# Turning the normalised rows of the second half on VectorE and through DRAM instead of on TensorE

## The reference

```python
h = _layernorm(x) * (1 + ca) + sa
x = x + ga * attention(h)          # q, k, v, rope, causal softmax, output projection
h = _layernorm(x) * (1 + cb) + sb
# ffn, for flat = h.reshape(2048, 512):
logits = flat @ router_weight.T + router_bias
scores = softmax(logits)
topk_w, topk_idx = top_k(scores, 8)
w_sum = topk_w.sum(-1, keepdims=True)
out = flat * w_sum + w_dense @ expert_bias
x = x + gb * out
```

## Time and profile before

| | |
|---|---|
| median of 3 runs | 1455.2 us (1454.89 to 1455.63) |
| profiled execution | 1455.76 us, span 1454.5 us |
| granted TensorE clock | 0.999 of full speed |
| busy, share of the span | PE 1432.3 us (98%), PEld 1210.8 (83%), DVE 1150.7 (79%), ACT 1008.6 (69%), POOL 1024.5 (70%) |
| DMA | 322.05 MB, mean 221 GB/s |

### The profile page before, as it was taken

The page is one execution under the profiler, slowest core; times in us unless marked ns, Lnnn a source line. Parts: engine busy times, 40 slices in busy tenths (PEclk is TensorE's granted clock), DMA queues, the critical chain, the costliest instruction groups (busy, mean ns, idle before and its releaser), DMA issues.

```text
span 1454.5 us, 24712 instructions
## 1 busy us (share of the span) xinstructions
PE 1432.3 (98%) x7150; PEld 1210.8 (83%) x7150; DVE 1150.7 (79%) x3541; ACT 1008.6 (69%) x2391; POOL 1024.5 (70%) x806
## 2 busy tenths in 40 slices
PE   7999999999999999999999999999999999999998
PEld 7887888888888888888888888888888888888886
DVE  5697777777877777777777787777779988898876
ACT  5686767667676666677676677677667676776674
POOL 3776866677676667677676677676588888887662
PEclk9999999999999999999999999999999999999999
DMA  9487667776666766676587668659878899888972
GB/s 307 164 238 236 223 185 201 240 219 187 185 219 199 214 211 217 195 219 195 179 234 218 213 182 219 191 174 267 229 231 261 270 293 262 284 248 277 269 233 68
DMA packets 215158, 322.05 MB, mean 221 GB/s; under 512 B 42512, under 2 KB 132464, under 8 KB 215024
## 3 DMA queue, kind: packets, MB, share of 16 engines
q1 hardware_dynamic: 214736, 320.39, 73.5%
q10 hardware_dynamic: 288, 0.07, 0.0%
HBM read 179.43 MB, written 140.95 MB: 220 GB/s over the span
## 4 chain that ended last, share of the span: by engine, by line
PE 87%; DVE 5%; POOL 3%; ACT 2%; issue 2%; DMA 1%; SPq 0%; DVEq 0%; ACTq 0%
PE bank_s L642 22%; PE bank_o L804 21%; PE bank_pv L766 14%; PE bank_s L708 13%; PE bank_s L674 5%; PE bank_s L659 5%; POOL PT_lo L1890 1%; PE bank_s L704 1%; PE bank_s L613 1%; PE bank_s L868 1%; DVE y L1581 1%; DVE blocks L1529 1%; PE bank_s L705 0%; POOL rot_c L1878 0%; DMA wc_scratch<-wc_out 0%
## 5 line engine op out<-in xcount | busy, mean ns | idle before, releaser
L1890 POOL TENSOR_TENSOR PT_lo<-PT_raw,PT_hi 128x640 fp32r<-128x640 f32 x247 | 384.2, 1577 | 29.1 <-ACT PT_hi L1152 29.1
L1138 ACT ACTIVATE probs<-probs,row_inv 128x512 f32<-128x512 f32 (+3 forms) x512 | 257.6, 553 | 195.0 <-DVE row_inv L1512 194.9
L1878 POOL TENSOR_TENSOR rot_c<-rot_c,rot_s 128x512 f32<-128x512 f32 x128 | 167.3, 1307 | 256.5 <-DVE rot_s L1469 256.5
L1131 ACT ACTIVATE probs<-probs,row_min 128x384 f32<-128x384 f32 (+3 forms) x512 | 281.6, 552 | 50.6 <-DVE row_min L1505 50.5
L1529 DVE STREAM_TRANSPOSE blocks<-probs 128x384 f32<-128x384 f32 x508 | 213.9, 447 | 22.4 <-ACT probs L1138 13.1
L708 PE MATMUL bank_s<-kT_both,qT_hi 128*128 128x512 f32 (+2 forms) x768 | 215.2, 341 | 1.7 <-issue 1.1
L1505 DVE CUSTOM_DVE_ANT_0 probs<-bank_s,mask 128x512 f32<-128x512 f32 (+2 forms) x384 | 205.3, 552 | 0.3
L1883 POOL TENSOR_TENSOR qT_lo<-rot_c,qT_hi 128x512 fp32r<-128x512 f32 x128 | 166.3, 1299 | 51.4 <-ACT qT_hi L1113 50.6
L804 PE MATMUL bank_o<-wo_lo,OT_hi 128*128 128x512 f32 x496 | 195.0, 393 | 0.0
L642 PE MATMUL bank_s<-hT_lo,wq_hi 128*128 128x512 f32 x480 | 193.5, 403 | 0.5
L804 PE MATMUL bank_o<-wo_hi,OT_hi 128*128 128x512 f32 x496 | 193.4, 390 | 0.0
(11 more groups left out here) (311 smaller groups left out, 3198.3 us busy)
## 6 DMA issues: line engine op xcount, KB each, us to landing
blocks<-blocks SPq DMA_DIRECT2D x127, 640.0 KB, 3.7
PT_raw<-blocks SPq DMA_DIRECT2D x500, 160.0 KB, 3.9
stage<-in_wq SPq DMA_DIRECT2D x32, 256.0 KB, 5.1
vblocks<-kv_raw SPq DMA_DIRECT2D x32, 256.0 KB, 5.4
kv_raw<-vblocks SPq DMA_DIRECT2D x128, 64.0 KB, 2.2
stage<-in_wo SPq DMA_DIRECT2D x32, 256.0 KB, 5.1
split_wq<-wq_hi SPq DMA_DIRECT2D x32, 256.0 KB, 5.4
split_wq<-wq_lo SPq DMA_DIRECT2D x32, 256.0 KB, 5.7
```

The lines of the kernel that those rows point to most:

```text
L1131: ins = act.activation(row(t, qt), row(t, qt), ACT.Exp, bias=row_min[m][:, qt:qt + 1], scale=-1.0, accum_out=row_sum[m][:, qt:qt + 1])
L1138: ins = act.activation(row(t, qt), row(t, qt), ACT.Copy, scale=row_inv[t % 2][:, qt:qt + 1])
L1878: pool.tensor_tensor(rot_c[:], rot_c[:], rot_s[:], ALU.add).then_inc(pool_a, 1)
L1890: pool.tensor_tensor(lo[:, at], raw_of(t)[:, at], hi[:, at].bitcast(F32), ALU.subtract).then_inc(pool_t, 1)
```

## The change

The four transposes of each of the 12 tiles leave TensorE. VectorE turns the normalised rows in 32x32 blocks (`turn_rows`) in the odd step after, SyncE stores them to a DRAM buffer (`store_turned`) and reads them back with the blocks in their places by four loads (`load_turned`). ScalarE modulates out of SBUF (`modulate_turned(n-2)`), a tile one even step later than before, at the same place. TensorE's logits move to the end of the even step, behind the values products, always into bank s1; the bias moves to the start of the next odd step on VectorE.

```diff
@@ tensor_program: scores, step
-                    if before is not None and logits_bank(t - 2) == f"s{qt}":
-                        tile_waits((bias, before - 2), last=EARLY_TILES - 1)
                     if qt == 1 and t - 2 in MOD_STEPS:
                         pe.wait_ge(dve_mod, MOD_READ[MOD_STEPS[t - 2]])
                     if qt == 1 and before is not None:
-                        tile_waits((h2T_copy, before - 1), last=EARLY_TILES - 1)
+                        tile_waits((mixed, before - 4), (bias, before - 2), last=EARLY_TILES - 1)
...
                 if n is not None:
                     pe.wait_ge(dve_s, score_read(t + 1, 0))
                     ffn_mix(early(n - 4), "s1")
-                    ffn_logits(early(n - 2), logits_bank(t))
                 if h % 2 == 0 and t > 2:
                     out_pair(t // 2 - 2, LOWER)
-                if n is not None:
-                    tile_waits((mixed, n - 4), last=EARLY_TILES - 1)
-                    ffn_transpose(early(n - 1), "s1")
                 if h % 2 == 0 and t > 0:
                     if t < ALL - 2:
                         values_pair(t // 2 - 1, UPPER)
                     else:
                         values_last_pair()
+                if n is not None:
+                    tile_waits((mixed, n - 4), last=EARLY_TILES - 1)
+                    ffn_logits(early(n - 2), "s1")
@@ scalar_program
+            def modulate_turned(i):
+
+                if 0 <= i < TILES:
+                    b = i // QT
+                    act.wait_ge(d_turned, TURNED * (i + 1))
+                    act.wait_ge(d_modT, COLUMNS)
+                    if i > 0:
+                        act.wait_ge(logits_done, i)
+                    hidden = turned[:].rearrange("p (i c a) -> p c i a", i=SUBS, a=SUB)
+                    for c in range(CH):
+                        ins = act.activation(h2T(i)[:, c * P:(c + 1) * P].rearrange("p (i a) -> p i a", a=SUB),
+                                             hidden[:, c], ACT.Identity,
                                              bias=modT_rows[:, 0, b, c:c + 1], scale=modT_rows[:, 1, b, c:c + 1])
                     ins.then_inc(h2T_copy, 1)
...
                 if n is not None:
-                    ffn_modulate(early(n - 1), "s1")
+                    modulate_turned(early(n - 2))
@@ vector_program
+            def turn_rows(i):
+                if 0 <= i < TILES:
+                    dve.wait_ge(normed, i + 1)
+                    if i > 0:
+                        dve.wait_ge(h2T_copy, i)
+                    dve.transpose(turned[:].rearrange("p (j c a) -> p c j a", j=SUBS, a=SUB),
+                                  normal[:].rearrange("p (c j b) -> p c j b", j=SUBS, b=SUB)).then_inc(transposed, 1)
...
+                if before is not None:
+                    ffn_bias(early(before - 2), "s1")
                 mask_and_max(t + 1, 0)
...
                 if before is not None:
+                    turn_rows(early(before - 1))
                     ffn_x1(early(before))
                     ffn_stats(early(before))
...
                     ffn_top(early(n - 3))
-                    ffn_bias(early(n - 2), logits_bank(t))
                     keep(early(n - 3))
@@ sync_program
+            def store_turned(i):
+                if 0 <= i < TILES:
+                    sp.wait_ge(transposed, i + 1)
+                    sp.dma_start(turned_d, turned[:]).then_inc(d_turned, 16)
+
+            def load_turned(i):
+                if 0 <= i < TILES:
+                    sp.wait_ge(d_turned, TURNED * i + 16)
+                    rows = turned_d.rearrange("(i b) (j x) -> j b i x", b=SUB, j=SUBS)
+                    for j in range(SUBS):
+                        to = turned[j * SUB:(j + 1) * SUB, :].rearrange("p (i x) -> p i x", i=SUBS)
+                        sp.dma_start(to, rows[j]).then_inc(d_turned, 16)
...
                     if 1 < t < ALL - 3:
                         load_transposed(t - 1)
+                    if ffn_tile(t - 1) is not None:
+                        store_turned(early(ffn_tile(t - 1) - 1))
                     load_transposed(t)
...
                 if moved(t + 1):
                     store_blocks(t + 1)
+                if ffn_tile(t - 1) is not None:
+                    load_turned(early(ffn_tile(t - 1) - 1))
```

More of the change, by code:

```diff
@@ L274, in build @@
         x_end = [gate1[1], shift2[1], scale2[1], Region(fourth[0]).take("x_end3", [P, HID])]
+        turned = Region(fourth[0]).take("turned", [P, HID])
         x_in = stage[0]
@@ L343, in build @@
         vblocks_d = [nc.dram_tensor(f"vblocks{i}", [P, SEQ], F32).ap() for i in range(2)]
+        turned_d = nc.dram_tensor("turned_scratch", [P, HID], F32).ap()
         v_raw = kv_raw[:].rearrange("p (i k a) -> p k i a", i=SUBS, a=SUB)
@@ L359, in q_bank @@
             return bank["pv" if t < 5 else {5: "o3", 6: "o3", 7: "pv"}.get(t, "s2" if third_first(t - 2) else "s3")]
-        def logits_bank(t):
-            return "s3" if third_first(t + 1) else "s2"
         def k_bank(u):
@@ L477, in build @@
         act_pro, act_comb, act_h = sem("act_pro"), sem("act_comb"), sem("act_h")
-        dve_pro, dve_mod, dve_ln, dve_xn, dve_h = (sem("dve_pro"), sem("dve_mod"), sem("dve_ln"), sem("dve_xn"),
-                                                   sem("dve_h"))
+        dve_pro, dve_mod, dve_ln, dve_h = sem("dve_pro"), sem("dve_mod"), sem("dve_ln"), sem("dve_h")
+        d_turned = sem("d_turned")
+        TURNED = 16 + 16 * SUBS
         act_xn = sem("act_xn")
@@ L1190, in ffn_modulate @@
                     act.wait_ge(d_modT, COLUMNS)
-                    if 0 < i < EARLY_TILES:
-                        act.wait_ge(logits_done, i)
                     if i == EARLY_TILES + 2:
@@ L1197, in ffn_modulate @@
                         ins = act.activation(h2T(i)[:, at], bank[ps][:, at], ACT.Identity,
+                                             bias=modT_rows[:, 0, b, c:c + 1], scale=modT_rows[:, 1, b, c:c + 1])
+                    ins.then_inc(h2T_copy, 1)
+            def modulate_turned(i):
[9 more added lines that the diff above has]
+                                             hidden[:, c], ACT.Identity,
                                              bias=modT_rows[:, 0, b, c:c + 1], scale=modT_rows[:, 1, b, c:c + 1])
@@ L2235, in load_column @@
                 sp.dma_start(to, src.rearrange("(c p) -> p c", p=P), allow_slow_non_contiguous=True).then_inc(d_modT, 16)
+            def store_turned(i):
[9 more added lines that the diff above has]
+                        sp.dma_start(to, rows[j]).then_inc(d_turned, 16)
             def load_end(j):
                 sp.wait_ge(shifted, 2 * QT)
+                if j == QT - 1:
+                    sp.wait_ge(h2T_copy, EARLY_TILES)
                 sp.dma_start(x_end[j][:], x_rows[EARLY_TILES + j]).then_inc(d_xend, 16)
```

## The result

| | before | changed |
|---|---|---|
| median of 6 runs each | 1455.81 us (1454.89 to 1457.78) | 1463.33 us (1460.08 to 1465.6) |
| ratio, with 95% interval | | 1.005 (1.0039 to 1.006) |
| span of the profiled execution | 1454.5 us | 1462.1 us |

The change makes the kernel 7.5 us slower. Forecast were 1461.2 us and slower by 0.4%; it is 0.5%, inside the range and inside rival A's own range.

What follows compares the result with a forecast made beforehand. The prediction took a dense TensorE stream as the bound, other engines finishing just in time. Its terms -5.0 + 8.3 + 2.7 = +6.0 gave 1461.8 us profiled, 1461.2 us as median, range 1454.5 to 1467.

Steps and rivals of the forecast that it cites:

- rival A: Logits on TensorE wait for ScalarE at t mod 4 = 2; 1458.5 to 1464.5 us; chance 0.56, the forecast itself.
- The transposes, -5.0: On TensorE, removing the four transposes of each of 12 tiles saves 0.42 us a tile, 5.0 us.
- rival E: Each transpose costs TensorE its whole 272 ns, so 13.1 us come back; with waits 1453.1 us; chance 0.03.
- The logits' wait, 8.3: TensorE waits before the logits for ScalarE's modulation in five steps of t mod 4 = 2, adding 8.3 us.
- The wait for GpSimd, 2.7: Values products, coming 1.30 us earlier, wait for GpSimd's low parts near t = 96, 112, 116, adding 2.7 us.
- VectorE's odd step, +0.22: Block transpose adds 0.67 us, an earlier start gives back 0.45: VectorE's odd step moves 0.22 us against TensorE.
- The DMAs, nothing: The store and loads of turned rows lie hidden beside other work: no cost, upper bound 6 us.
- Rival B: The transfer becomes a bound: half a microsecond more for each of 12 tiles, 1467 us; chance 0.19.
- Rival C: Late TensorE gives GpSimd and VectorE time: GpSimd wait vanishes, logits' wait halves, about 1455.5 us; chance 0.15.
- Rival D: Faster: transposes go and ScalarE reaches the modulation early enough everywhere, 1450.2 us; chance 0.07.

Runs made afterwards that it cites:

- Experiment 8: Kernel before without the 12 tiles' transposes, ScalarE modulating straight from untransposed normalised rows, logits at their old place: 1451.11 us, ratio 0.9965.
- experiment 1: Changed kernel with ScalarE's modulation moved ahead of the key split in steps t mod 4 = 2: 1454.49 us, ratio 0.999 to the kernel before.
- experiment 6: Changed kernel with one 512-column activation for the modulation instead of four of 128: 1458.35 us, ratio 1.0012 to the kernel before.
- experiment 11: Changed kernel with VectorE's small two-source subtraction replaced by a one-source instruction with accumulator: 1461.07 us, ratio 1.0042 to the kernel before.
- experiment 2: Changed kernel with VectorE adding the logits' bias ahead of the output's low part: 1463.96 us, ratio 1.0056 to the kernel before.
- experiment 7: Changed kernel with VectorE turning only 32 of 512 columns in tiles 1 to 11: 1461.32 us, ratio 1.0038 to the kernel before.
- experiment 5: Changed kernel without the DRAM store and four loads of the turned rows: 1461.66 us, ratio 1.0037 to the kernel before.
- experiment 10: Changed kernel with the modulation ahead of the key split and no DRAM store or loads of turned rows: 1454.24 us, ratio 0.9992 to the kernel before.
- experiment 9: Changed kernel with the modulation ahead of the key split and VectorE turning only 32 columns in tiles 1 to 11: 1452.33 us, ratio 0.9982.

## Why the prediction was right, and where it was not

The steps of the profiled executions by kind, t = 94 to 119, changed minus before:

| steps | forecast | measured |
|---|---|---|
| t mod 4 = 2 (94 to 118) | 8.3 - 6 x 0.42 = +5.8 | +5.5 |
| t mod 4 = 0 (96 to 116) | 2.7 - 6 x 0.42 = +0.2 | -0.5 |
| odd (95 to 119) | 0 | +4.4 |
| sum | +6.0 | +9.4 |

(With t = 119 the sum is 9.4; up to its start, the stretch, it is 8.6. The rest of the execution was 1.8 us shorter than in the profile of before: the part ahead of t = 94, whose code did not change, by 2.0, of which 1.6 are the fall of the clock at t = 5 that the profile of before holds. The profiles of the experiments have the start of t = 94 between 1048.98 and 1051.91 us. Without the two falls the two executions differ by 7.8 us.)

- **The transposes, -5.0: right.** Experiment 8 has 5.1 us by the runs and 3.9 in the stretch. The start times held, not the durations: 48 x 0.272 = 13.1 (rival E) would have shown as a ratio of 0.991. By the 275 ns of the Trainium skill, "TensorE: Matmul & The Clock Gate", Part 4 (PE-mode transpose), an estimate would have been 13.2; the measurement decides.
- **The logits' wait, 8.3: right in place and cause, 7.4 in size.** Five steps, none worth a name at t = 118 (0.1). Experiments 1 and 6 show the cause: it goes with the modulation's place and with its length. The modulation grew by 0.15 us a tile (1.48 to 1.63) where I took 0.12. The estimate from the Trainium skill, "VectorE: DVE Perf Modes", section "The TRN2 errata", was 0.17.
- **The wait for GpSimd, 2.7: 2.0 measured**, at t = 96 (0.51) and 116 (0.31) as named, not at 112; instead small ones at 98, 104, 108 and 110. The margins read from single steps shifted with VectorE, so the sum was near and the places were half right.
- **VectorE's odd step, +0.22 in the stalled steps: the step that failed.** I had VectorE free "about 1.0" behind the scores' start. In the odd steps with t mod 4 = 3 it is (1.12), but for t = 119. In those with t mod 4 = 1 it is 1.34 to 1.89 from t = 101 on, at t = 119 2.26, and there the bias, which now stands between the values products and the second tile of the scores, is waited for: t = 101, 105, 109, 113, 117 grow by 0.94, 0.42, 0.90, 0.92 and 0.40 and t = 119 by 0.76, 4.3 us together, of which the list of waits shows 2.9 (short ones are folded into a group's duration). The prediction had no wait of TensorE for the bias at all. I had counted what moved on VectorE, but not what its two-source instructions meet on GpSimd when everything is 1 us earlier. In experiment 11, without one of these instructions, what was lost at t = 105, 117 and 119 is gone; what was lost at 101, 109 and 113 stayed, each time behind the next such instruction, held up in its place. Neither that instruction nor the bias's place (experiment 2) nor the 0.7 us of the turn (experiment 7) is the cause alone.
- **The clock, +1.5 less 0.5: not forecast.** Step 99 grew by 1.0 net. Other odd steps won: 95 and 111 are 0.57 and 0.55 shorter, and there the first maximum comes 1.1 us behind the scores instead of 1.8 and 1.9.
- **The DMAs, nothing: right as far as the runs can tell** (1.7 us by the medians in experiment 5, 0.25 in experiment 10, both inside the intervals). Rival B is out: 1.2 us more of waiting on ScalarE, not 6.
- **Rival C, the stall feeds back: out in the changed kernel** (all five waits stand), but a mirror of it is at work: whatever was taken away in experiments 2, 7 and 11 came back in part in a later step.
- **Rival D named the right lever.** It needed ScalarE 1.1 us earlier; experiment 1 gives it that by its place in ScalarE's order, with the keys as late as before. Even so the gain is 1 us and not 5. How the other 4 split is not shown. By the ratios of experiments 1, 9 and 8 (0.999, 0.9982, 0.9965) about 1.2 us are VectorE's turn and 2.5 are left when it is short; by the stretches (287.83, 285.16, 283.12) it is 2.7 and 2.0, but experiment 10, with the whole turn, has 285.27. In the part that is left the values products still come 0.88 earlier: they wait 2.1 us for GpSimd's low parts in experiment 9 and 0.2 in 8.

That 1461.2 was near 1463.3 is in part luck. The even steps were forecast 1.0 us too long and the odd ones 4.4 too short: 2.9 of these are the waits for the bias, less what other odd steps won, and 1.5 the clock's fall, which the fall in the profile of before happens to cancel. Without the falls it is 7.8 us against the 6.0 of the forecast.

## What to carry to other kernels

When work is moved between engines that run in order and finish just in time, the saved matmul time is only a ceiling: list for each step what would be late next, the floor, before counting the gain. Look in the timeline of the receiving engine for an idle gap and put the new work there: here one group of four activations ahead of a wait instead of behind it was worth almost 9 us (1463.3 to 1454.5). The two-source instructions of VectorE cost here what GpSimd happened to be doing; price them by their longest duration in the trace, not by their shortest. Before two profiles are subtracted, look in both for the falls of the clock: one of them can lie in code that did not change.

## What was not expected of the hardware

- A 128x64 subtraction on VectorE took 0.23 us or up to 1.30 us, the long ones ending 0.08 to 0.09 us behind a GpSimd instruction; an operation of that size with one source took 0.278 to 0.281 us in all 12 places in experiment 11.
- A single idle stretch of 1.4 us on TensorE was followed, 2 us later, by 3.2 us at a granted clock of 0.50 (1.2 GHz), for 1.5 us; four like it were not. The stretch of 1.8 us at t = 5 was followed by such a fall in 2 of 14 profiled executions. Why in these is open.
- Four activations of 128x128 with two operands for each partition took 1.63 us out of SBUF and 1.48 out of PSUM; a block transpose of 128x512 on VectorE 0.707 us out of SBUF.
